# A three-layer feature-interaction tower on one core: the row sums of layer 2 taken from VectorE and made by ScalarE's accumulator, 16 columns at a time

## Chip, cores and metric

The kernel runs on one core of one Trainium2 chip. The metric is the device time of one execution in microseconds (us), median of the runs shown. All data are 32-bit floats.

## The reference, cut to what matters

For 1024 samples, 32 embeddings of 16 numbers are gathered from 32 tables (`e`, 1024 x 32 x 16). Three layers follow, each made of products of `e` with the layer before, contracted with a weight tensor. Each layer gives one sum over the 16 numbers (`d`) of its relu to a small MLP.

```python
    x0 = embeddings; xk = x0; outs = []
    for W in (W0, W1, W2):
        xk = jax.nn.relu(jnp.einsum('bmd,bhd,mhk->bkd', x0, xk, W))   # k = 64 maps
        outs.append(jnp.sum(xk, axis=2))
    z = jnp.concatenate(outs, axis=1)                 # 1024 x 192
    h = jnp.concatenate([z, dense_ctx], axis=1)       # 1024 x 208
    h = jnp.maximum(h @ W_top1 + b_top1, 0.0)         # 512
    h = jnp.maximum(h @ W_top2 + b_top2, 0.0)         # 256
    y = h @ W_top3
```

Layer 2 is the last of the three: its relu is not used again, only its sums are.

## The kernel before

The columns are the 1024 x 16 pairs (sample, number), worked in 16 steps of 1024 columns (64 samples). Half a step is 512 columns (32 samples, HALF_B), the width of one PSUM bank.

**Gather and spread.** GpSimd (POOL) gathers the embeddings of step s+2 during step s (`gather`, L247). SyncE (SP) stores them to HBM as rows (`store_rows`, L187), waits for the store, and then loads, on one queue, `x0g` of that step (L197) and 16 tiles `x0bc` of 128 x 1024 (L214, two tiles a semaphore). They go round in 24 slots.

**A layer.** For each of 16 tiles an elementwise product with the layer before is made, by VectorE for two tiles at once (L286, 128 x 2048) or, for the last 3 tiles of layers 1 and 2, by POOL (L260). TensorE contracts the products into one PSUM bank of 128 x 512 (`y_ps`, L413: the upper and lower 64 rows are the two halves of the step). Two such banks alternate. Layer 0 has only 4 tiles, and the squares made by ScalarE (L360). VectorE's products go through a ring of four (`prod`); the wait for a free place is `products_used`.

**After a layer** (`finish` on ScalarE, ACT): for layers 0 and 1, four copies of the relu to PSUM for VectorE (L370), the relu of the whole bank into SBUF (L374, 128 x 512), and four copies to SBUF for POOL (L379). For layer 2 only L374 runs. VectorE then makes the sums: `sums(s, l)`, one reduction of 128 x 512 to 128 x 32 (L314).

**Order written out by hand.** On VectorE, in step s: layer 1 of s; layer 0 of s+1; sums of layer 0 of s; sums of layer 2 of s-1; layer 2 of s; sums of layer 1 of s. On TensorE: layer 1 of s, layer 0 of s+1, layer 2 of s. On ScalarE: `place_x0g(s+1)` (L355, which waits for the load of x0g, and for which VectorE's layer 0 waits), `square(s+1)` (L360), `finish(s,1)`, `finish(s+1,0)`, `finish(s,2)`. On POOL, in step s: 3 tiles of layer 1 and 3 of layer 2, with 16 gathers between them. In the last two steps POOL takes 5 and 4 tiles.

**End.** `mlp_input(c)` on VectorE copies the sums of 8 steps into place with six copies (L326). The MLP jobs run on TensorE (L466, L467, L473) and ScalarE (L388 to L392) in the order of `MLP`: jobs (1,0,j) before layer 2 of the last step, and after it (2,0,0), (2,0,1), (1,1,0) to (1,1,3), and the rest. The jobs (1,1,j) wait for `mlp_input(1)`. On ScalarE all jobs after the first four stand behind `finish(LAST, 2)`.

Of the kernel before, what the change touches and what calls it, by code (L numbers as in the profile page):

```python
# [8 lines left out]
ACT = mybir.ActivationFunctionType  # L9
# [5 lines left out]
DIM = 16  # L15
# [12 lines left out]
HALF_B = STEP_B // 2  # L28
# [27 lines left out]
def groups_of(s, l):  # L56
    tiles = list(range(TILES - POOL_COUNT[s][l - 1])) if l else list(range(LOW))
    return [tiles[i:i + GROUP] for i in range(0, len(tiles), GROUP)]
# [7 lines left out]
def before(x):  # L66

    return sum(len(groups_of(*y)) for y in STAGES[:NUMBER[x]])


def after(x):
    return before(x) + len(groups_of(*x))
# [15 lines left out]
LAST = STEPS - 1  # L88


def slot(s, j):
    return (TILES * s + j) % SLOTS


def cin_tower_kernel(nc, table, ids, id_offset, dense_t, w0_a, w0_b, w0_sq, w1, w2,
                     wt1_a, wt1_b, bt1, wt2, bt2, wt3, x0_rows, out):
    with ExitStack() as ctx:
        def sb(name, shape, dt=F32):
            return ctx.enter_context(nc.sbuf_tensor(name, shape, dt))
# [4 lines left out]
        def sem(name):  # L104
            return ctx.enter_context(nc.semaphore(name))
# [16 lines left out]
        relu = sb("relu", [P, 3, HALF])  # L122
        z = sb("z", [P, 3, STEPS * HALF_B])
# [45 lines left out]
        relu_done = [sem(f"relu{l}_done") for l in range(3)]  # L169
# [6 lines left out]
        def y_bank(x):  # L176
            return y_ps[NUMBER[x] % 2]
# [100 lines left out]
        @block.vector  # L278
        def _(dve):
            def product(n, count, tiles, x, h=None):  # L280

                if n >= RING and h != 1:
                    dve.wait_ge(products_used, n - RING + 1)
                cols = slice(0, PAIR) if h is None else slice(HALF * h, HALF * (h + 1))
                right = x[:].rearrange("p h c -> p (h c)")[:, cols]
                made = dve.tensor_tensor(prod[:, n % RING, 0:count, cols], tiles[:, :, cols],  # L286
                                         right.unsqueeze(1).to_broadcast([P, count, right.shape[1]]), ALU.mult)
                if h != 0:
                    made.then_inc(products, 1)

            def layer0(s):
                dve.wait_ge(x0g_placed, s + 1)
                for g, group in enumerate(groups_of(s, 0)):
                    dve.wait_ge(bc_in[g], 32 * (s + 1))
                    at = slot(s, group[0])
                    product(before((s, 0)) + g, GROUP, x0bc[:, at:at + GROUP, :], x0g_ps)

            def layer(s, l, x):
                for g, group in enumerate(groups_of(s, l)):
                    if l == 1:  # L300
                        dve.wait_ge(bc_in[g], 32 * (s + 1))
                    n, at, count = before((s, l)) + g, slot(s, group[0]), len(group)
                    tiles = x0bc[:, at:at + count, :]
                    if g == 0:

                        for h in range(2):
                            dve.wait_ge(spread_done[l - 1], 4 * s + 2 * h + 2)
                            product(n, count, tiles, x, h)
                    else:
                        product(n, count, tiles, x)  # L310

            def sums(s, l):
                dve.wait_ge(relu_done[l], s + 1)
                dve.tensor_reduce(z[:, l, s * HALF_B:(s + 1) * HALF_B],  # L314
                                  relu[:, l, :].rearrange("p (b d) -> p b d", d=DIM), AX_X,
                                  ALU.add).then_inc(summed[l], 1)

            def mlp_input(c):
                steps = STEPS // 2
                for l in range(3):  # L320
                    dve.wait_ge(summed[l], steps * (c + 1))
                for l, dst in enumerate((zt_a[0:MAPS, :], zt_a[MAPS:P, :], zt_b[0:MAPS, :])):
                    dst = dst[:, HALF * c:HALF * (c + 1)].rearrange("p (s h b) -> p s h b", h=2, b=HALF_B)
                    for h in range(2):
                        src = z[MAPS * h:MAPS * (h + 1), l, steps * HALF_B * c:steps * HALF_B * (c + 1)]
                        dve.tensor_copy(dst[:, :, h, :],  # L326
                                        src.rearrange("p (s b) -> p s b", b=HALF_B)).then_inc(zt_ready, 1)

            dve.wait_ge(weights_in, 16 * 5)
            dve.tensor_tensor(w0s_sb[:], w0a_in, w0b_in, ALU.add).then_inc(w0_ready, 1)  # L330

            dve.tensor_scalar(wsq_sb[:], wsq_in, 1.0 / QUART, None, ALU.mult).then_inc(w0_ready, 1)

            layer0(0)
            for s in range(STEPS):
                layer(s, 1, x1_ps)
                if s < LAST:
                    layer0(s + 1)
                sums(s, 0)
                if s > 0:  # L340
                    sums(s - 1, 2)
                if s == LAST:
                    mlp_input(0)
                layer(s, 2, x2_ps)
                sums(s, 1)
            sums(LAST, 2)
            mlp_input(1)

        @block.scalar
        def _(act):  # L350
            def place_x0g(s):
                act.wait_ge(x0g_in, 16 * (s + 1))
                if s > 0:
                    act.wait_ge(products, after((s - 1, 0)))
                act.activation(x0g_ps[:].rearrange("p h c -> p (h c)"), x0g[:], ACT.Copy).then_inc(x0g_placed, 1)  # L355

            def square(s):
                if s > 0:
                    act.wait_ge(squares_used, s)
                act.activation(squares[:], x0g[:], ACT.Square).then_inc(squared, 1)  # L360

            def finish(s, l, x=None, x_sb=None):

                ps = y_bank((s, l))

                act.wait_ge(products_used, after((s, l)))
                if x is not None:
                    for h in range(2):
                        for copy in range(2):
                            act.activation(x[MAPS * copy:MAPS * (copy + 1), h, :], ps[MAPS * h:MAPS * (h + 1), :],  # L370
                                           ACT.Relu).then_inc(spread_done[l], 1)
                if s > 0:
                    act.wait_ge(summed[l], s)
                act.activation(relu[:, l, :], ps[:], ACT.Relu).then_inc(relu_done[l], 1)  # L374
                if x is not None:
                    act.wait_ge(relu_done[l], s + 1)
                    for h in range(2):
                        for copy in range(2):
                            act.activation(x_sb[MAPS * copy:MAPS * (copy + 1), HALF * h:HALF * (h + 1)],  # L379
                                           relu[MAPS * h:MAPS * (h + 1), l, :], ACT.Copy).then_inc(copied[l], 1)  # L380

            def mlp(jobs):
                for n in jobs:
                    layer, c, j = MLP[n]
                    act.wait_ge(mlp_mm, n + 1)
                    ps = mlp_ps[n % MLP_BANKS]
                    if layer == 1:
                        act.activation(h1[:, j, :], ps, ACT.Relu, bias=bt1_sb[:, j:j + 1]).then_inc(mlp_act, 1)  # L388
                    elif layer == 2:
                        act.activation(h2[:, j, :], ps, ACT.Relu, bias=bt2_sb[:, j:j + 1]).then_inc(mlp_act, 1)  # L390
                    else:
                        act.activation(y_sb[:, HALF * c:HALF * (c + 1)], ps[0:1, :], ACT.Copy).then_inc(mlp_act, 1)  # L392

            place_x0g(0)
            square(0)
            finish(0, 0, x1_ps, x1_sb)
            for s in range(STEPS):
                if s < LAST:
                    place_x0g(s + 1)
                    square(s + 1)  # L400
                finish(s, 1, x2_ps, x2_sb)
                if s < LAST:
                    finish(s + 1, 0, x1_ps, x1_sb)
                else:
                    mlp(range(MLP_EARLY))
                finish(s, 2)
            mlp(range(MLP_EARLY, len(MLP)))

        @block.tensor
        def _(pe):  # L410
# [6 lines left out]
            def wait_bank(x):  # L417

                n = NUMBER[x]
                if n >= 2:  # L420
                    s, l = STAGES[n - 2]
                    pe.wait_ge(relu_done[l], s + 1)

            def layer0(s):
                wait_bank((s, 0))
# [107 lines left out]
```

## Time and profile before

| | us |
|---|---|
| median of 3 runs | 644.31 (643.63 to 645.4) |
| the profiled execution | 642.9 |
| its span, first to last instruction | 641.1 |
| VectorE busy in it | 558.1 |
| TensorE busy in it | 559.1 |
| GpSimd busy in it | 488.4 |
| ScalarE busy in it | 224.6 |

The span lies inside the profiled execution's own time; 1.8 us lie around it. The median is 1.4 us above that execution. Shares of busy time are means over a filling part at the start (the first gathers), a repeating middle of about 35 us a step, and the MLP at the end, so the middle and the end have to be read apart.

### The profile page before, as it was taken

Reading aid. Unit: us, or ns where it says so; the run is one execution under the profiler, and the core shown is the slowest. Engines: PE = TensorE matmul, PEld = TensorE weight load, DVE = VectorE, ACT = ScalarE, POOL = GpSimd, SP = SyncE. Lnnn points to the kernel's source line nnn. Section 1 sums busy time; section 2 is a strip of 40 time slices with the busy share of each in tenths; the row PEclk is TensorE's granted clock in tenths of the full one; section 3 lists DMA queues with packets and bytes.
Section 4 is the critical chain, followed back from the end, with each engine's and each line's share of the span. In section 5 each row is a group of like instructions: output and inputs, shape, how many; then the busy total and the mean of one; then the engine's idle time right before and its main releaser. Section 6 shows DMA issues by size and latency. Waiting matters only on the chain.

```text
span 641.1 us, 6648 instructions
## 1 busy us (share of the span) xinstructions
PE 559.1 (87%) x2440; PEld 179.6 (28%) x2440; DVE 558.1 (87%) x346; ACT 224.6 (35%) x351; POOL 488.4 (76%) x364
## 2 busy tenths in 40 slices
PE   0047998999999998999999899999899999989998
PEld 0012232332323232323232232222232233323342
DVE  0047998999999999999999999999999999898810
ACT  0032607053341616160524425161606143340422
POOL 6756798879888888978788888888797979675500
PEclk9998999999999999999999999999999999999999
DMA  3298857677876758676778778675767687772000
GB/s 104 45 384 299 305 189 291 242 297 266 305 271 246 272 206 297 235 288 222 294 267 298 267 260 288 225 280 214 294 232 282 253 300 265 295 268 72 1 0 0
DMA packets 52835, 150.94 MB, mean 235 GB/s; under 512 B 9697, under 2 KB 17377, under 8 KB 52802
## 3 DMA queue, kind: packets, MB, share of 16 engines
q1 hardware_dynamic: 44610, 148.40, 62.8%
q0 software_dynamic: 8192, 2.11, 2.5%
q8 instruction: 19, 0.31, 0.2%
q14 instruction: 14, 0.11, 0.0%
HBM read 147.33 MB, written 3.15 MB: 235 GB/s over the span
## 4 chain that ended last, share of the span: by engine, by line
DVE 47%; DMA 16%; PE 15%; issue 13%; POOL 7%; SPq 2%; ACT 0%; DVEq 0%; POOLq 0%
DVE prod L286 43%; DMA x0bc<-x_rows 12%; PE y_ps L413 10%; POOL emb L247 6%; DVE z L314 4%; PE x0g_ps L473 2%; DMA x_rows<-emb 2%; DMA emb<-table,row_sb 2%; SPq L214 1%; PE x_ps L473 1%; POOL pool_prod L260 1%; PE x0g_ps L466 1%; PE x0g_ps L467 1%; PE x_ps L467 1%; PE x_ps L466 1%
## 5 line engine op out<-in xcount | busy, mean ns | idle before, releaser
L286 DVE TENSOR_TENSOR prod<-x0bc,x_ps 128x2048 f32<-128x2048 f32 (+1 forms) x252 | 456.2, 1879 | 8.6 <-ACT x_ps L370 7.2
L413 PE MATMUL y_ps<-prod,w_sb 128*64 128x512 f32 x1640 | 383.2, 597 | 36.6 <-DVE prod L286 36.6
L247 POOL DMA_INDIRECT emb<-table,row_sb x256 | 245.0, 957 | 65.4 <-issue 63.4
L260 POOL TENSOR_TENSOR pool_prod<-x0bc,x_sb 128x1024 f32<-128x1024 f32 x102 | 242.3, 2381 | 50.4 <-ACT x_sb L379 39.3
L413 PEld LDWEIGHTS y_ps<-prod,w_sb 128*64 128x64 f32 x1640 | 115.2, 137 | 287.3 <-issue 225.4
L413 PE MATMUL y_ps<-pool_prod,w_sb 128*64 128x512 f32 x408 | 105.1, 595 | 5.1 <-POOL pool_prod L260 5.1
L370 ACT ACTIVATE x_ps<-y_ps 64x512 f32<-64x512 f32 x128 | 73.0, 570 | 87.8 <-PE y_ps L413 85.2
L286 DVE TENSOR_TENSOR prod<-x0bc,x0g_ps 128x2048 f32<-128x2048 f32 x32 | 72.3, 2281 | 34.6 <-DMA x0bc<-x_rows 31.0
L379 ACT ACTIVATE x_sb<-relu 64x512 f32<-64x512 f32 x128 | 80.4, 628 | 3.4
L374 ACT ACTIVATE relu<-y_ps 128x512 f32<-128x512 f32 x48 | 28.7, 597 | 147.1 <-PE y_ps L413 146.3
L355 ACT ACTIVATE x0g_ps<-x0g 128x1024 f32<-128x1024 f32 x16 | 16.4, 1028 | 156.9 <-DMA x0g<-x_rows 156.9
L413 PE MATMUL y_ps<-prod,w0s_sb 128*64 128x512 f32 x256 | 60.3, 611 | 1.5 <-DVE prod L286 1.4
L413 PE MATMUL y_ps<-squares,wsq_sb 128*64 128x512 f32 x64 | 17.4, 623 | 35.6 <-ACT squares L360 35.6
L413 PEld LDWEIGHTS y_ps<-pool_prod,w_sb 128*64 128x64 f32 x408 | 29.0, 137 | 64.9 <-issue 51.7
L314 DVE TENSOR_REDUCE z<-relu 128x32 f32<-128x512 f32 x48 | 31.2, 675 | 6.4 <-ACT relu L374 6.4
L413 PEld LDWEIGHTS y_ps<-prod,w0s_sb 128*64 128x64 f32 x256 | 18.3, 140 | 41.7 <-issue 29.7
L413 PEld LDWEIGHTS y_ps<-squares,wsq_sb 128*64 128x64 f32 x64 | 4.6, 141 | 44.2 <-issue 44.2
L360 ACT ACTIVATE squares<-x0g 128x1024 f32<-128x1024 f32 x16 | 16.7, 1041 | 0.0
L473 PE MATMUL x0g_ps<-x0bc 128*128 128x512 f32 x24 | 10.7, 596 | 0.0
L330 DVE TENSOR_TENSOR w0s_sb<-pool_prod 128x256 f32<-128x256 f32 x1 | 0.4, 425 | 8.5 <-DMA w_sb<-w 8.5
L473 PEld LDWEIGHTS x0g_ps<-x0bc 128*128 128x128 f32 x24 | 4.5, 190 | 6.1 <-issue 6.1
L390 ACT ACTIVATE x0bc<-x0g_ps,bt_sb 128x512 f32<-128x512 f32 x3 | 2.1, 688 | 8.5 <-PE x0g_ps L473 8.5
(27 smaller groups left out, 45.4 us busy)
## 6 DMA issues: line engine op xcount, KB each, us to landing
x0bc<-x_rows SPq DMA_DIRECT2D x256, 512.0 KB, 6.6
x0g<-x_rows SPq DMA_DIRECT2D x16, 512.0 KB, 4.7
emb<-table,row_sb POOLq DMA_INDIRECT x256, 5.0
x_rows<-emb SPq DMA_DIRECT2D x16, 128.0 KB, 2.1
w_sb<-w SPq DMA_DIRECT2D x2, 512.0 KB, 4.5
x_rows<-emb SPq DMA_DIRECT2D x16, 64.0 KB, 2.0
x0bc<-wt SPq DMA_DIRECT2D x1, 512.0 KB, 5.3
x0bc<-wt_a SPq DMA_DIRECT2D x1, 256.0 KB, 4.0
```

The costliest lines, as they stand in the source:

```text
L247: pool.indirect_dma_start(emb[:, turn, DIM * n:DIM * (n + 1)], None, table, bass.IndirectOffsetOnAxis(row_sb[:, at:at + 1], 0)).then_inc(g ...
L260: pool.tensor_tensor(pool_prod[:, n % POOL_RING, :], x0bc[:, slot(s, j), :], x[:], ALU.mult).then_inc(pool_products, 1)
L286: made = dve.tensor_tensor(prod[:, n % RING, 0:count, cols], tiles[:, :, cols], right.unsqueeze(1).to_broadcast([P, count, right.shape[1]] ...
L314: dve.tensor_reduce(z[:, l, s * HALF_B:(s + 1) * HALF_B], relu[:, l, :].rearrange("p (b d) -> p b d", d=DIM), AX_X, ALU.add).then_inc(summ ...
L355: act.activation(x0g_ps[:].rearrange("p h c -> p (h c)"), x0g[:], ACT.Copy).then_inc(x0g_placed, 1)
L360: act.activation(squares[:], x0g[:], ACT.Square).then_inc(squared, 1)
L370: act.activation(x[MAPS * copy:MAPS * (copy + 1), h, :], ps[MAPS * h:MAPS * (h + 1), :], ACT.Relu).then_inc(spread_done[l], 1)
L374: act.activation(relu[:, l, :], ps[:], ACT.Relu).then_inc(relu_done[l], 1)
L379: act.activation(x_sb[MAPS * copy:MAPS * (copy + 1), HALF * h:HALF * (h + 1)], relu[MAPS * h:MAPS * (h + 1), l, :], ACT.Copy).then_inc(cop ...
L413: made = pe.matmul(ps[MAPS * h:MAPS * (h + 1), :], w, moving[:, HALF * h:HALF * (h + 1)], start=first, stop=final)
L466: pe.matmul(ps, wt1a_sb[:, out_f], zt_a[:, b], start=True, stop=False)
L473: made = pe.matmul(ps[0:rows, :], w[:, k, :], x[:, k, :], start=k == 0, stop=k == ks - 1)
```

## The change

VectorE's 16 reductions of layer 2 are taken out. ScalarE no longer makes one relu of 128 x 512 for layer 2; it makes 32 relus of 128 x 16, each of one sample's 16 columns, and each also writes the sum of its columns to one column of `z` (`accum_out`). The waits that counted one relu a step count 32 for layer 2, and the wait of layer 2's relu for VectorE's last sum falls away.

```diff
             def mlp_input(c):
                 steps = STEPS // 2
-                for l in range(3):
+                for l in range(2):
                     dve.wait_ge(summed[l], steps * (c + 1))
+                dve.wait_ge(relu_done[2], HALF_B * steps * (c + 1))
...
                 sums(s, 0)
-                if s > 0:
-                    sums(s - 1, 2)
                 if s == LAST:
                     mlp_input(0)
                 layer(s, 2, x2_ps)
                 sums(s, 1)
-            sums(LAST, 2)
             mlp_input(1)
...
+                if l == 2:
+
+                    for b in range(HALF_B):
+                        act.activation(relu[:, l, DIM * b:DIM * (b + 1)], ps[:, DIM * b:DIM * (b + 1)], ACT.Relu,
+                                       accum_out=z[:, l, s * HALF_B + b:s * HALF_B + b + 1]).then_inc(relu_done[l], 1)
+                    return
                 if s > 0:
                     act.wait_ge(summed[l], s)
                 act.activation(relu[:, l, :], ps[:], ACT.Relu).then_inc(relu_done[l], 1)
...
-                    pe.wait_ge(relu_done[l], s + 1)
+                    pe.wait_ge(relu_done[l], (HALF_B if l == 2 else 1) * (s + 1))
```

## Rows read from the trace of the kernel before

**Rows 1.** The page: span, and busy time of each engine.

```profile
span 641.1 us, 6648 instructions
PE 559.1 (87%) x2440; PEld 179.6 (28%) x2440; DVE 558.1 (87%) x346; ACT 224.6 (35%) x351; POOL 488.4 (76%) x364
```

**Rows 2.** Timeline of VectorE, one middle step (start, length in us, engine, line).

```profile
314.64 1.27 DVE L314 TENSOR_REDUCE z<-relu 128x32 f32<-128x512 f32 x2
315.83 14.46 DVE L286 TENSOR_TENSOR prod<-x0bc,x_ps 128x1024 f32<-128x1024 f32 x8
...
330.80 14.46 DVE L286 TENSOR_TENSOR prod<-x0bc,x_ps 128x1024 f32<-128x1024 f32 x8
345.33 4.68 DVE L286 TENSOR_TENSOR prod<-x0bc,x0g_ps 128x2048 f32<-128x2048 f32 x2
```

**Rows 3.** Timeline of ScalarE, the same step; in brackets the idle time before.

```profile
312.74 2.35 ACT L370 ACTIVATE x_ps<-y_ps 64x512 f32<-64x512 f32 x4 [4.34 <-PE y_ps L413]
...
332.70 0.60 ACT L374 ACTIVATE relu<-y_ps 128x512 f32<-128x512 f32 x1 [8.76 <-PE y_ps L413]
341.40 1.03 ACT L355 ACTIVATE x0g_ps<-x0g 128x1024 f32<-128x1024 f32 x1 [8.10 <-DMA x0g<-x_rows]
```

**Rows 4.** ScalarE's instructions grouped: busy us, mean ns of one, idle before.

```profile
L379 ACT ACTIVATE x_sb<-relu 64x512 f32<-64x512 f32 x128 | 80.4, 628 | 3.4
...
L374 ACT ACTIVATE relu<-y_ps 128x512 f32<-128x512 f32 x48 | 28.7, 597 | 147.1 <-PE y_ps L413 146.3
L360 ACT ACTIVATE squares<-x0g 128x1024 f32<-128x1024 f32 x16 | 16.7, 1041 | 0.0
```

**Rows 5.** SyncE's queue: the loads of x0bc that follow a store.

```profile
337.25 5.18 SPq L214 DMA_DIRECT2D x0bc<-x_rows  x6
```

**Rows 6.** Chain that ended last, around 345 us: a load.

```profile
339.19 8.50 DMA x0bc<-x_rows
```

**Rows 7.** Line L214, third and fourth load: first of the twelve steps.

```profile
L214 SPq DMA_DIRECT2D x0bc<-x_rows x2: 588/726/863, 128.3 to 128.9; - x2
...
DMA to landing us min/median/max: 7.2/7.7/8.2
```

**Rows 8.** The same, last of the twelve steps.

```profile
L214 SPq DMA_DIRECT2D x0bc<-x_rows x2: 602/656/709, 513.9 to 514.6; - x2
...
DMA to landing us min/median/max: 6.6/7.0/7.3
```

**Rows 9.** Timeline of GpSimd: its first tile of layer 2.

```profile
318.41 2.37 POOL L260 TENSOR_TENSOR pool_prod<-x0bc,x_sb 128x1024 f32<-128x1024 f32 x1 [1.26 <-ACT x_sb L379]
```

**Rows 10.** Timeline of TensorE: the start of layer 2.

```profile
318.31 1.94 PE L413 MATMUL y_ps<-prod,w_sb 128*64 128x512 f32 x8 [1.33 <-DVE prod L286]
```

**Rows 11.** Timeline of VectorE: last two steps.

```profile
555.75 2.29 DVE L286 TENSOR_TENSOR prod<-x0bc,x0g_ps 128x2048 f32<-128x2048 f32 x1 [2.35 <-issue]
...
593.55 13.40 DVE L286 TENSOR_TENSOR prod<-x0bc,x_ps 128x1024 f32<-128x1024 f32 x7 [2.83 <-ACT x_ps L370]
```

**Rows 12.** Timeline of the end: ScalarE.

```profile
613.32 0.60 ACT L374 ACTIVATE relu<-y_ps 128x512 f32<-128x512 f32 x1 [12.91 <-PE y_ps L413]
```

**Rows 13.** Timeline of the end: VectorE.

```profile
613.95 0.69 DVE L314 TENSOR_REDUCE z<-relu 128x32 f32<-128x512 f32 x1 [6.40 <-ACT relu L374]
614.77 1.88 DVE L326 COPY x0bc<-z 64x256 f32<-64x256 f32 x6
```

**Rows 14.** Timeline of the end: TensorE.

```profile
613.20 7.13 PE L473 MATMUL x0g_ps<-x0bc 128*128 128x512 f32 x16
620.17 1.02 PE L466 MATMUL x_ps<-x0bc 128*128 128x512 f32 x2
```

**Rows 15.** TensorE early in the kernel, after an idle stretch.

```profile
55.67 1.50 PE L413 MATMUL y_ps<-pool_prod,w_sb 128*64 128x512 f32 x4 [3.66 <-POOL pool_prod L260]
56.94 3.22 PE L413 MATMUL y_ps<-prod,w_sb 128*64 128x512 f32 x8
```

**Rows 16.** Busy time and TensorE's granted clock (PEclk, after POOL) in two stretches there.

```profile
57.00:58.00 1.00, 1.00 (x6) 0.39 (x4) 1.00 (x1) 0.00 (x0) 1.00 (x1) 0.50 0.81 49
...
60.00:61.00 1.00, 1.00 (x8) 0.42 (x6) 0.72 (x1) 0.12 (x1) 0.98 (x2) 1.00 0.99 352
```

## The prediction

> **What bounds the kernel now.** I read the page first: VectorE and TensorE are both busy 87% of the 641.1 us span, ScalarE 35% [rows 1]. Two engines look equal there, so the next view is the timeline of one middle step on VectorE. It shows products, sums and products again with no gap: from 315.83 the layer-2 products last to 330.29, the layer-1 products run 330.80 to 345.26, layer 0 starts at 345.33 [rows 2]. TensorE in the same step idles 1.33 us before layer 2, waiting for VectorE's product [rows 10]. So VectorE sets the pace in the middle, and the work that the change removes stands in its queue. ScalarE idles 8.10 us between the relu of layer 2 and the placing of x0g, for which it waits on a load [rows 3].
>
> VectorE is not alone, though. The chain that ended last runs at 345 us through a load of x0bc of 8.50 us, issued at 339.19 and landed at 347.69 [rows 6], 0.2 us after VectorE could have used it: the second of its two layer-0 products would have started at 345.33 + 2.20 = 347.53 (two of them take 4.68 us instead of the usual 4.47 [rows 2]). The loads of a step start only when POOL's gathers are stored [rows 5], and POOL starts that series when ScalarE hands it x_sb [rows 9]. So a second loop, POOL, store, load, runs just beside VectorE.
>
> At the end, TensorE runs MLP jobs from 613.20 to 620.17 while ScalarE and VectorE finish layer 2 by 616.65 [rows 12 to 14]: 3.52 us of cover.
>
> **Removed from VectorE, middle.** Two sums in a row take 1.27 us, and products start 1.19 us after the first of them; a lone one takes 0.69 and would give 0.60 [rows 2, 13]. So one removed sum brings the layer-2 products 0.59, say 0.6 us, forward. Fifteen sums go before the last step's end. Which of them lie on the path?
> - The one of step 15 (before the products of 593.55) does not: VectorE idles 2.83 us there for x_ps [rows 11]. Gain 0.
> - The one of step 13 does not: the layer 0 after it already idles 2.35 us before 555.75 [rows 11], called issue, but the second load of that step lands just then. It is late by the second loop, whose start lies before the removed sum. Gain 0.
> - The one of step 14 does: TensorE is next, and it waits for VectorE at that place as in [rows 10]. 0.6.
> - Twelve are left, steps 1 to 12: 12 x 0.6 = 7.2 us at best.
>
> **What the second loop takes back.** x_sb, with which POOL's series starts, comes from layer 1, whose products precede the removed sum. So POOL, stores and loads are not 0.6 us earlier when VectorE is, and the margin of the fourth load before the second layer-0 product shrinks by 0.6 in each step. In the first of the twelve steps it lands at 128.9 + 8.2 = 137.1 [rows 7] with the product at 137.6, a margin of 0.5; in the last at 514.6 + 7.3 = 521.9 [rows 8] with the product at 522.8, 0.9. The twelve, worked out the same way: 0.5, 0.5, 0.8, -0.1, 0.7, 0.7, -0.2, 0.3, 0.3, -0.3, 0.7, 0.9. Where the margin is under 0.6 only the margin is gained: 0.5 + 0.5 + 0.6 + 0 + 0.6 + 0.6 + 0 + 0.3 + 0.3 + 0 + 0.6 + 0.6 = 4.6. A stall in one step leaves the next margin larger by its length, since x_sb precedes the stall; followed through the twelve, this gives back up to 0.7 (5.3). I take 5.0, with step 14 **5.6 us gained**. Ends: 7.8 if the loads come earlier too, 3 if they jitter more. POOL keeps up: of its 1.26 us of idle [rows 9] 0.6 goes.
>
> **Added on ScalarE: what one small relu costs.** No row shows a 16-column activation or one with its sum written out. From 512 to 1024 columns an SBUF activation goes from 628 to 1041 ns, 0.81 ns a column [rows 4]; the PSUM relu of 512 takes 597 ns [rows 4], so 16 columns take 597 - 496 x 0.81 = 195 ns. Four copies take 2.35 us [rows 3], some 20 ns apart beyond their length. A small relu alone: at least 0.2 us. The written-out sum is a single column that can only go out when the 16 are through. Nothing excludes that it hides in the gap (0), and as a second instruction it can hardly cost more than a small activation of its own (0.2). So one costs 0.2 to 0.41 us, and 32 cost 6.6 to 13.1. Between them I take half an instruction, 0.3 us, **9.6 us for 32**: one column is less than a full small activation, but a write that follows another has never been free in these rows.
>
> The row shows that 512 columns cost 597 ns, of which 180 or so are fixed [rows 4]; cut in 32 the fixed part is paid 32 times. The Trainium skill says the same against this change (Advanced Engine Details and Errata, The Read-Write Bubble): large tiles of 512 or 1024 elements, because latency shows between instructions. On the size it differs: by ScalarE: Activation LUTs (What ACT_TABLE_LOAD costs) 16 columns take 186 + 13 = 199 ns with immediate operands, and consecutive activations overlap by 93, which would make it an estimate of 106 ns each and 3.4 us for 32. The rows above show no overlap, only gaps.
>
> **Beside what it lies in the middle.** From 332.70 ScalarE is idle, but for the 0.6 us relu, until 341.40 [rows 3]: 8.7 us. 9.6 puts the placing of x0g at 342.4 instead, its end (1.03 later) at 343.4. VectorE needs it at 345.33 [rows 2]. So up to 345.3 - 1.1 - 332.7 = 11.5 us (0.36 each) cost nothing; queued behind it are the placing, the square and finish(s,1), whose PSUM bank is full only about 15 us after the relu (4.34 us of idle before 312.74 [rows 3]). TensorE's own wait for the bank of layer 2 comes later than the square, so it is behind the same work. Cost 0.
>
> **Added at the end.** After 613.32 stand 32 relus instead of 0.60 us of relu and 0.69 of sum [rows 12, 13]. Then the six copies, 1.88 us and 0.1 of waiting: the sums are in place at 613.3 + 9.6 + 2.0 = 624.9. The jobs (1,1,j) started at 620.17 [rows 14]. The cover of 3.52 us is used up, **4.7 us lost**. In general 32p - 4.9, with p the cost of one.
>
> TensorE idles these 4.7 us. Early in the kernel it idled 3.66 us [rows 15] and then ran at a granted clock of 0.50 (1.2 GHz), with 1.00 (2.4 GHz) again by 60 us [rows 16]; 8 matmuls took 3.22 us where they take 1.94 [rows 10, 15], and four 1.50 where they take 1.03: 1.8 us in all. The end is a chain through TensorE, so I add **1.8 us lost**. (The Trainium skill, TensorE: Matmul & The Clock Gate, states that idleness halves the array's clock until work has gone on for a time; the trace agrees with its 0.50.)
>
> **The sum.** -5.6 + 4.7 + 1.8 = +0.9 us. The profiled execution took 642.9, so 643.8; the median shown is 1.4 above it, so 644.3 + 0.9 = **645.2 us**. That is within 0.3% (1.9 us), about what a measurement of this kernel can tell from no change.
>
> **Rivals.**
> - *ScalarE becomes the bound (slower).* If one costs over 0.36 us, the placing of x0g is late in every step and layer 0 with it. At 0.37 (11.8 us) it is 0.3 to 0.4 late each step, the gain falls from 5.6 to about 2.5, the end costs 6.9 + 1.8: +6, 650.5. At 0.41 it is 1.6 us late, net of the removed sum 1.0 in each of twelve steps, and 10.1 at the end: +22, 666. For it: two dependent writes an activation. Against: it needs more than three quarters of a full instruction for the sum.
> - *The small ones are cheap (faster).* At 0.2 us, 6.6 for 32, the end costs 1.7, the idle stretch is too short to resemble [rows 15], and the gain of 5.6 stands: -3.9, 640.4. The overlap that the skill states is this rival's rule taken further; at that price the end would lie wholly in cover and the time would be 638.7.
> - *The gain does not come.* If the loads' loop takes back nearly all (gain 1.0), the end's 6.5 stands: +5.5, 649.8. For it: three of twelve margins are below zero already. Against: five are 0.7 or more.
> - That the sums stay on VectorE is excluded by the diff.
>
> **From these to the numbers.** The forecast 0.45 (one costs 0.25 to 0.36; 643 to 647), ScalarE bound 0.22, cheap 0.2, no gain 0.13. The range reaches from the cheap case, 640.4, to past the milder bound case, 651. Faster: the cheap case and a little of the forecast's edge, less its weak part, 0.2. Slower: bound, no gain, and little else, 0.36. Same 0.44.
>
> **What the changed kernel's profile would show.** On ScalarE, 512 activations of 128x16, and perhaps as many rows for the sums: the stretch from the first to the last of a step should be 9.6 us. VectorE should have 32 reductions, steps of about 34.5 us instead of 34.94, and more idle time on x0bc loads (about 2.5 us more). TensorE should idle 4 to 5 us before the first matmul of (1,1,0), with the clock at 0.5 behind it. The placing of x0g should follow the last small relu without a gap. Wrong would be: a stretch of under 8 or over 11.5 us; idle time on VectorE before layer 0 that ends with the placing; a clock that stays at 1.00 at the end (1.8 us less).

## The result, and the profile after

The changed kernel takes 638.83 us (median of 4 runs, 638.44 to 639.81) against 644.86 of the kernel before, run beside it: ratio 0.991, 95% interval 0.989 to 0.993, 4 to 7 us faster. Its profiled execution took 638.9, with a span of 637.1, against 642.9 and 641.1: 4.0 us less in this pair. I had forecast 645.2 and no measurable change; the time lies below the whole range.

The page first: its span, and busy time by engine.

```profile
span 637.1 us, 7625 instructions
...
PE 563.1 (88%) x2440; PEld 178.9 (28%) x2440; DVE 548.7 (86%) x330; ACT 302.5 (47%) x1359; POOL 488.3 (77%) x364
```

VectorE has 16 instructions and 9.4 us less than in [rows 1]. ScalarE has 1008 more: 496 relus, and 512 of a kind that was not there. Its groups (busy us, mean ns of one, idle before):

```profile
L373 ACT ACTIVATION_READ_ACCUMULATOR relu<-y_ps 128x1 f32 x512 | 84.7, 315 | 0.2
L373 ACT ACTIVATE relu<-y_ps 128x16 f32<-128x16 f32 x512 | 84.5, 287 | 144.3 <-PE y_ps L417 144.3
```

So the sum is a second instruction. The means of 287 and 315 ns mislead. The timeline of ScalarE shows it (start, length):

```profile
296.60 0.17 ACT L373 ACTIVATE relu<-y_ps 128x16 f32<-128x16 f32 x1
296.66 0.19 ACT L373 ACTIVATION_READ_ACCUMULATOR relu<-y_ps 128x1 f32 x1
296.75 0.17 ACT L373 ACTIVATE relu<-y_ps 128x16 f32<-128x16 f32 x1
...
301.28 0.41 ACT L373 ACTIVATE relu<-y_ps 128x16 f32<-128x16 f32 x1
301.34 0.44 ACT L373 ACTIVATION_READ_ACCUMULATOR relu<-y_ps 128x1 f32 x1
305.38 1.03 ACT L353 ACTIVATE x0g_ps<-x0g 128x1024 f32<-128x1024 f32 x1 [3.61 <-DMA x0g<-x_rows]
```

Each row starts before the one ahead of it has ended, and the rows grow longer, from 0.17 to 0.44 us, while the distance from one relu to the next stays 0.155. What counts is the distance of the starts: 0.06 to the read, 0.09 to 0.10 to the next relu. For the step that answers to [rows 3], line L373 between 325 and 340 us:

```profile
L373 ACT ACTIVATE relu<-y_ps x32: 165/284/413, 331.8 to 336.8; 128x16 f32<-128x16 f32 x32
L373 ACT ACTIVATION_READ_ACCUMULATOR relu<-y_ps x32: 192/311/441, 332.0 to 336.9; 128x1 f32 x32
```

From 331.8 to 336.9 + 0.44, the end of the last row, are 5.5 us for all 32, not 9.6. The placing of x0g still waits for its load, 2.89 us after them, in place of 8.10:

```profile
340.18 1.03 ACT L353 ACTIVATE x0g_ps<-x0g 128x1024 f32<-128x1024 f32 x1 [2.89 <-DMA x0g<-x_rows]
```

VectorE, two products of layer 0 and what follows (answers to [rows 2]):

```profile
308.52 2.28 DVE L286 TENSOR_TENSOR prod<-x0bc,x0g_ps 128x2048 f32<-128x2048 f32 x1
312.13 2.29 DVE L286 TENSOR_TENSOR prod<-x0bc,x0g_ps 128x2048 f32<-128x2048 f32 x1 [1.32 <-DMA x0bc<-x_rows]
314.33 0.68 DVE L314 TENSOR_REDUCE z<-relu 128x32 f32<-128x512 f32 x1
314.93 14.46 DVE L286 TENSOR_TENSOR prod<-x0bc,x_ps 128x1024 f32<-128x1024 f32 x8
```

One sum now, and products 0.60 us after it; but 1.32 us of idle before the second product, which waits for a load. VectorE's waits between 100 and 540 us (total, times, longest), first of the kernel before:

```profile
DVE prod L286 <- DMA x0bc<-x_rows: 1.0, 2, 0.8
DVE prod L286 <- issue: 0.9, 1, 0.9
```

and of the changed kernel:

```profile
DVE prod L286 <- DMA x0bc<-x_rows: 5.5, 7, 1.9
DVE prod L286 <- issue: 1.0, 2, 0.7
```

A wait called issue stands before the same products, with no releaser named; I count it with the loads, as in the prediction. So 6.5 us of idle in place of 1.9 in this pair, 4.6 us more. Single executions differ in this, though. In the same stretch the trace of a kernel with all sums on VectorE and small relus added has 4.2 us, and three further traces with layer 2's sums gone from VectorE have 5.3, 4.9 and 4.5 us (all from the experiments below; traces of the first job, disturbed as told there, are left out). Two executions with the sums on VectorE have 3.1 us in the mean, four without them 5.3: 2.2 us more.

The end, TensorE first (answers to [rows 14]), then VectorE (to [rows 13]):

```profile
608.46 7.13 PE L477 MATMUL x0g_ps<-x0bc 128*128 128x512 f32 x16
616.10 1.10 PE L470 MATMUL x_ps<-x0bc 128*128 128x512 f32 x2 [0.51 <-DVE x0bc L327]
```

```profile
614.07 1.88 DVE L327 COPY x0bc<-z 64x256 f32<-64x256 f32 x6 [11.27 <-ACT relu L373]
```

TensorE enters the MLP's last part 4.74 us earlier than before (608.46 against 613.20), and waits 0.51 us in it, not 4.7. Of the 4.74, 0.74 was there before any sum was removed: the products of step 0's layer 2 start at 68.38 us, in the kernel before at 69.12. Over the traces of this study that start lies anywhere from 67.8 to 71.7 us. Its granted clock there (the figure 1.00 behind the busy times):

```profile
616.00:620.00 4.00, 3.90 (x9) 1.81 (x10) 0.00 (x0) 1.19 (x3) 0.00 (x0) 1.00 0.00 0
```

### The profile page after: what moved, and what is told of

The parts are those of the page before. It is cut to its first block, busy times and chain, and to the rows that moved or that the text cites. A ratio compares the mean times of both kernels' runs of the same rounds, so it can differ in the third digit from the quotient of the medians.

```text
span 637.1 us, 7625 instructions
## 1 busy us (share of the span) xinstructions
PE 563.1 (88%) x2440; PEld 178.9 (28%) x2440; DVE 548.7 (86%) x330; ACT 302.5 (47%) x1359; POOL 488.3 (77%) x364
## 4 chain that ended last, share of the span: by engine, by line
DVE 36%; PE 24%; DMA 19%; issue 10%; POOL 8%; SPq 2%; ACT 1%; DVEq 0%; POOLq 0%
DVE prod L286 34%; PE y_ps L417 20%; DMA x0bc<-x_rows 15%; POOL emb L247 6%; DVE z L314 2%; DMA emb<-table,row_sb 2%; DMA x_rows<-emb 2%; POOL pool_prod L260 1%; SPq L214 1%; PE x_ps L477 1%; ACT relu L373 1%; PE x0g_ps L477 1%; PE x_ps L470 1%; PE x0g_ps L470 1%; PE x0g_ps L471 1%
## 5 line engine op out<-in xcount | busy, mean ns | idle before, releaser
L260 POOL TENSOR_TENSOR pool_prod<-x0bc,x_sb 128x1024 f32<-128x1024 f32 x102 | 242.3, 2382 | 45.7 <-ACT x_sb L383 36.3
L373 ACT ACTIVATE relu<-y_ps 128x16 f32<-128x16 f32 x512 | 84.5, 287 | 144.3 <-PE y_ps L417 144.3
L373 ACT ACTIVATION_READ_ACCUMULATOR relu<-y_ps 128x1 f32 x512 | 84.7, 315 | 0.2
L417 PE MATMUL y_ps<-prod,w0s_sb 128*64 128x512 f32 x256 | 61.6, 617 | 5.4 <-DVE prod L286 5.4
L314 DVE TENSOR_REDUCE z<-relu 128x32 f32<-128x512 f32 x32 | 21.6, 676 | 0.0
L378 ACT ACTIVATE relu<-y_ps 128x512 f32<-128x512 f32 x32 | 19.1, 597 | 0.8
L327 DVE COPY x0bc<-z 64x256 f32<-64x256 f32 x12 | 3.4, 286 | 11.6 <-ACT relu L373 11.3
L477 PE MATMUL x0g_ps<-x0bc 128*128 128x512 f32 x24 | 10.7, 597 | 0.0
```

Source lines behind the costliest of these rows:

```text
L260: pool.tensor_tensor(pool_prod[:, n % POOL_RING, :], x0bc[:, slot(s, j), :], x[:], ALU.mult).then_inc(pool_products, 1)
L314: dve.tensor_reduce(z[:, l, s * HALF_B:(s + 1) * HALF_B], relu[:, l, :].rearrange("p (b d) -> p b d", d=DIM), AX_X, ALU.add).then_inc(summ ...
L373: act.activation(relu[:, l, DIM * b:DIM * (b + 1)], ps[:, DIM * b:DIM * (b + 1)], ACT.Relu, accum_out=z[:, l, s * HALF_B + b:s * HALF_B + ...
L417: made = pe.matmul(ps[MAPS * h:MAPS * (h + 1), :], w, moving[:, HALF * h:HALF * (h + 1)], start=first, stop=final)
L477: made = pe.matmul(ps[0:rows, :], w[:, k, :], x[:, k, :], start=k == 0, stop=k == ks - 1)
```

## Experiments

Ratios are to the kernel before, run on the same chip in the same job, with their 95% intervals. The changed kernel's is 0.991. The edits are to the changed kernel unless another is named.

### The addition and the removal, each alone

**Nobody sums layer 2.** ScalarE makes one relu of 128x512 as before, the MLP reads layer 1's sums twice.

```diff
-                    for b in range(HALF_B):
-                        act.activation(relu[:, l, DIM * b:DIM * (b + 1)], ..., accum_out=z[...])
+                    act.activation(relu[:, l, :], ps[:], ACT.Relu).then_inc(relu_done[l], 1)
...
-                        src = z[MAPS * h:MAPS * (h + 1), l, ...]
+                        src = z[MAPS * h:MAPS * (h + 1), min(l, 1), ...]
```

> Leaves work out: nobody sums layer 2; ScalarE makes one relu of 128x512, and the MLP gets layer 1's sums in place of layer 2's. It is the removal from VectorE without the addition to ScalarE. Theory A (the small relus are covered by ScalarE's idle time in the middle and cost only what sticks out of TensorE's MLP jobs at the end, 0.5 us): within 1.5 us of the changed kernel, 637 to 639 us, middle steps alike, with VectorE idle 4 to 7 us on loads of x0bc between 100 and 540 us. Rival B (the small relus cost something in the middle too, for example by the later placing of x0g): 3 us or more faster than the changed kernel.

0.991 (0.988 to 0.995), in a job where the kernel before itself took 646.6. Repeated in another job:

> The kernel in which nobody sums layer 2 (the MLP gets layer 1's sums in its place), once more. Theory A: 0 to 1.5 us less than the changed kernel, 637 to 639 us. Rival B: 635 us or less; then the small relus cost 3 us or more in the changed kernel.

637.05 us, 0.990 (0.987 to 0.993). Both ratios are the changed kernel's. So the 512 small relus with their sums cost nothing that can be told from none.

**The small relus added, VectorE's sums kept** (edit to the kernel before):

```diff
+                if l == 2:
+                    for b in range(HALF_B):
+                        act.activation(relu[:, l, DIM * b:DIM * (b + 1)], ps[:, DIM * b:DIM * (b + 1)], ACT.Relu,
+                                       accum_out=z_acc[:, b:b + 1]).then_inc(relu_done[l], 1)
+                    return
```

> The kernel before, with layer 2's relu made as 32 relus of 16 columns whose sums are written out into a tile that nobody reads; VectorE still makes the sums. It is the addition to ScalarE without the removal from VectorE. Theory A (5.0 us, covered in the middle; at the end 613.2 + 5.1 + 0.8 + 1.9 = 621.0 against 620.2): +0.5 to +1.5 us, not to be told from the kernel before. Rival B (the small relus slow something else in the middle): +3 us or more.

1.000 (0.999 to 1.002). At the end of its profile TensorE waits, as expected:

```profile
625.45 1.10 PE L472 MATMUL x_ps<-x0bc 128*128 128x512 f32 x2 [1.23 <-DVE x0bc L327]
```

So the gain is the removal's.

**Small relus without a sum written out** (the kernel before with `accum_out` left away in the edit above):

> The kernel before with layer 2's relu cut into 32 relus of 16 columns without an accumulator; VectorE still makes the sums. It shows the price of a small relu alone. Theory A (a relu and the writing out of its sum take 0.156 us from one to the next, of which 0.09 is the relu): 32 take about 3 us; the middle does not change; the end has 613.3 + 3.0 + 0.8 + 1.9 = 619 against 620.2, still covered; time as before, within 1 us. Rival B (consecutive activations overlap only when an accumulator write stands between them; alone each takes the 0.195 us of my prediction): 32 take 6.2 us, and the end is 2 us later, +2 us.

1.001 (0.998 to 1.003). Line L376 in one step:

```profile
L376 ACT ACTIVATE relu<-y_ps x32: 178/372/578, 338.5 to 340.5; 128x16 f32<-128x16 f32 x32
```

31 distances in 2.0 us (2.0 to 2.1 in the steps at 89, 125, 161 and 197 us too): one relu each 0.065 us, less than the 0.09 that theory A gave it and a third of the 0.195 of my prediction. The last row ends at 341.1, 2.6 us after the first start. The Trainium skill (ScalarE: Activation LUTs, What ACT_TABLE_LOAD costs) has back-to-back activations overlap, an estimate of 106 ns for 16 columns: right in direction, and the measured 65 ns decides. The gap between instructions that the Trainium skill holds against small tiles (Advanced Engine Details and Errata, The Read-Write Bubble) does not show in these rows, which overlap. Large tiles are cheaper all the same: the 32 take 2.6 us, one relu of 512 columns 0.60 [rows 4].

### The end

```diff
-                if l == 2:
+                if l == 2 and s < LAST:
...
+            dve.wait_ge(relu_done[2], HALF_B * LAST + 1)
+            dve.tensor_reduce(z[:, 2, LAST * HALF_B:], relu[:, 2, :].rearrange("p (b d) -> p b d", d=DIM), AX_X,
+                              ALU.add).then_inc(summed[2], 1)
             mlp_input(1)
```

> The changed kernel, with step 15's layer 2 done the old way: one relu of 128x512, then VectorE's reduction. Theory A (32 relus at the end cost only what exceeds TensorE's cover, 0.5 us): TensorE goes into the jobs (1,1,j) without a wait, the profile's stretch from the last matmul of layer 2 to the end is 0.4 to 0.6 us shorter; the time is 0 to 1 us less, not to be told from the changed kernel. Rival B (the 5 us of relus count in full at the end): 4 us less.

637.85 us, 0.990 (0.987 to 0.994), not to be told from the changed kernel. In the profile TensorE no longer waits:

```profile
608.72 7.13 PE L483 MATMUL x0g_ps<-x0bc 128*128 128x512 f32 x16
615.69 1.02 PE L476 MATMUL x_ps<-x0bc 128*128 128x512 f32 x2
```

From 608.72 to the end of the span, 636.6, are 27.9 us, as before the change (613.20 to 641.1), against 28.6 in the changed kernel (608.46 to 637.1). The end costs 0.7 us, not 6.5. The timed runs cannot show so little, but the traces agree: from the start of VectorE's last products of layer 2 to the end are 47.5 to 47.6 us in the kernel before, here and where nobody sums, and 48.3 in the changed kernel and its copy with one increment a step (below).

### How much ScalarE could take

My cover of 11.5 us a step in the middle was not tested by 5 us of work. So the relus were made again into tiles that nobody reads, in steps 0 to 14 (`range(2)` in the tripled kernel):

```diff
+                    if s < LAST:
+                        for r in range(1):
+                            for b in range(HALF_B):
+                                act.activation(relu_more[:, r, DIM * b:DIM * (b + 1)], ps[:, DIM * b:DIM * (b + 1)],
+                                               ACT.Relu, accum_out=z_more[:, r, b:b + 1]).then_inc(relu_done[l], 1)
```

**Doubled:**

> The changed kernel with layer 2's 32 relus and sums made twice in steps 0 to 14 (the second time into tiles that nobody reads), once in step 15. Theory A (cover of 11.5 us in the middle): 64 take 10.0 us, the placing of x0g comes 1 to 2 us later than in the changed kernel and still before VectorE needs it; time unchanged within 1.5 us. Rival B (the cover is the 8.1 us until x0g lands, and what exceeds it shows): 1 to 1.5 us a step, +15 to +20 us.

1.007 (1.003 to 1.012), 10 us above what the changed kernel's ratio would give, and neither theory's number.

**Tripled:**

> The same three times, 96 relus and sums, 15.0 us. Theory A: 3.5 us over the cover of 11.5 in each of some 14 steps, less the idle time on loads that it swallows (5 us): VectorE waits before layer 0 for the placing of x0g, +40 to +49 us, 680 to 688. Rival B (cover 8.1): 7 us a step, +95. Rival C (other work moves into the gap, so less shows): under +30.

787.3 us, 1.217: no theory's number either. ScalarE's timeline there shows pauses among the relus:

```profile
285.17 0.19 ACT L380 ACTIVATION_READ_ACCUMULATOR relu_more<-y_ps 128x1 f32 x1
285.74 0.18 ACT L380 ACTIVATE relu_more<-y_ps 128x16 f32<-128x16 f32 x1 [0.37 <-issue]
286.44 0.20 ACT L380 ACTIVATION_READ_ACCUMULATOR relu_more<-y_ps 128x1 f32 x1 [0.52 <-issue]
```

Rows that had followed at 0.155 us a pair now came at about 0.7. I took the semaphore increments, one a relu, for the cause, and left one a step, behind the loop:

```diff
-                    ... accum_out=...).then_inc(relu_done[l], 1)
+                    made = act.activation(..., accum_out=...)
+                    made.then_inc(relu_done[l], 1)
```

> The kernel with layer 2's relus and sums made three times in steps 0 to 14, but with one semaphore increment a step, at the last relu, in place of 96. In the run with 96 increments ScalarE went from 0.156 us a pair to 0.7 us a pair after some 70 pairs, and the time was 787 us. Theory A (the increments' way is what backs up): all 96 pairs go at 0.156, 15.0 us, and the time is the 680 to 688 us expected for the cover of 11.5 us. Rival B (the supply of instructions to ScalarE is what runs dry, or the writes of one column): the pauses stay, 780 us or more.

> The same two times, one increment a step. Theory A: 10.0 us, inside the cover of 11.5 us: the time of the changed kernel, 637 to 641 us, and no late copies to PSUM for layer 2. Rival B: as the doubled kernel with all increments, 650 us or more.

Tripled 699.3 us, 1.083 (1.082 to 1.085); doubled 638.6, 0.991 (0.989 to 0.994). That looked like proof, but the two pairs had run in different jobs. The same kernels with all increments, repeated:

> The kernel that makes layer 2's relus and sums three times in steps 0 to 14, each with its own semaphore increment, once more in another job. Theory A (96 increments in a row back up whatever the chip): 780 us or more again, with ScalarE's pauses of 0.35 to 1.2 us. Rival B (that job's chip was the cause): about 699 us, as with one increment a step.

> The kernel that makes them three times, a third time. Theory A: 697 to 701 us; the 787 us was of that one job. Rival B: about 787 us again; then the kernel has two ways to run.

> The kernel that makes layer 2's relus and sums twice in steps 0 to 14, each with its own increment, once more. Theory A (the first job's chip delayed it; the cover is 11.5 us): 637 to 641 us, as with one increment a step. Rival B (the increments delay it): 648 us or more again.

698.8 (1.085, 1.083 to 1.088) and 699.6 (1.086, 1.082 to 1.090) tripled; 637.6 (0.991, 0.988 to 0.994) doubled. So the increments alone were not the cause, and my theory fell; a kernel with one increment was not run in the first job. The pauses belonged to that job, in which the kernel before was slower too (646.6 against 643.6 to 644.9 in the others). Nor was it a matter of small relus alone. In the four traces of that job ScalarE's first copies to PSUM, before any small relu, start at 48.9 to 49.9 us, in all others at 43.7 to 45.7. The record gives chip 1 for this job and for that of the 699.3 us. What delayed ScalarE there stays open; of that job only the two ratios near 1 that were repeated or that agree with others are used here, and the 65 ns a relu.

**One increment a step in the changed kernel itself:**

> The changed kernel with one semaphore increment a step for layer 2's relus in place of 32. Theory A (32 never back up): the changed kernel's time, within 1 us, 0.155 us a pair. Rival B (they cost something already): 2 us or more faster.

638.8, 0.992 (0.990 to 0.995): no effect.

With the disturbance gone, the cover is seen. The tripled kernel with one increment, line L378, and VectorE before layer 0:

```profile
L378 ACT ACTIVATE relu_more<-y_ps x64: 435/616/617, 328.0 to 338.3; 128x16 f32<-128x16 f32 x64
L378 ACT ACTIVATION_READ_ACCUMULATOR relu_more<-y_ps x64: 463/642/645, 328.1 to 338.4; 128x1 f32 x64
L378 ACT ACTIVATE relu<-y_ps x32: 167/290/426, 322.8 to 327.9; 128x16 f32<-128x16 f32 x32
```

```profile
340.10 4.49 DVE L288 TENSOR_TENSOR prod<-x0bc,x0g_ps 128x2048 f32<-128x2048 f32 x2 [4.70 <-ACT x0g_ps L355]
```

From 322.8 to 338.4 + 0.64 are 16.2 us, and 16.2 - 11.5 = 4.7: the idle time of VectorE, which ends with the placing of x0g (4.7 to 5.0 in the middle steps). The doubled relus, 10.7 us in the trace with one increment (329.4 to 340.1), fit and cost nothing. The 699 us is more than the 680 to 688 expected because 96 relus take 16.2, not 15.0 us.

### Where the rest of the gain went

**One gather moved ahead of POOL's tiles of layer 2**, in the changed kernel and in the one before:

```diff
-GATHERS_AFTER = {1: [1, 1, 8], 2: [1, 1, 4]}
+GATHERS_AFTER = {1: [1, 1, 9], 2: [1, 1, 3]}
```

> The changed kernel with one gather moved ahead of POOL's tiles of layer 2 in each step (9 and 3 in place of 8 and 4), so that the store and the loads of a step start up to 1.25 us earlier. Theory A (what was not gained in the middle, 2 to 5 us, was taken back by the loop of gathers, stores and loads): VectorE's idle time on x0bc loads between 100 and 540 us falls from 6.5 us to under 2; 3 to 4.5 us faster than the changed kernel. Rival B (POOL itself has only 0.65 us of idle left, so the gather moved ahead delays its tiles and x_sb's use by 0.6, and TensorE waits for POOL's products): under 1.5 us faster or slower, with new waits of TensorE on POOL. Rival C (the loads are late by transfer speed, not by their start): no change of that idle time.

634.8 us, 0.985 (0.983 to 0.988), 4 us under the changed kernel's 638.8. VectorE's waits between 100 and 540 us:

```profile
DVE prod L286 <- DMA x0bc<-x_rows: 2.5, 2, 1.9
DVE prod L286 <- issue: 0.3, 1, 0.3
```

2.8 us in place of 6.5, and less than in any of the four traces named above (4.5 to 6.5): in the changed kernel VectorE does wait for the loop of gathers, store and loads. (I had expected under 2.)

> The same move of one gather in the kernel before. Theory A: there VectorE idles only 1.9 us on loads between 100 and 540 us, so 1 to 2 us at most are gained, which the measurement can't tell from none. Rival B: the same gain as in the changed kernel, 3 us or more; then the second loop bounded the kernel before as well.

641.8, 0.996 (0.994 to 0.998), 2.4 us less: between the two theories. Its profile has 3.3 us of such idle in that stretch, not less than before, so where its gain sits is not shown. And since the same move gives 2.4 us here and 4 us there, with intervals wider than the difference, the times do not show how much of the 4 us the removed sums had lost to the loop.

**Layer 0's sums by ScalarE too**, behind the copies to POOL:

```diff
-                sums(s, 0)
...
+                if l == 0:
+                    for b in range(HALF_B):
+                        act.activation(relu_out[:, DIM * b:DIM * (b + 1)], relu[:, 0, DIM * b:DIM * (b + 1)], ACT.Relu,
+                                       accum_out=z[:, 0, s * HALF_B + b:s * HALF_B + b + 1]).then_inc(summed[0], 1)
```

> The changed kernel, with layer 0's sums made by ScalarE too: 32 relus of 16 columns of the relu in SBUF, behind the copies to POOL, with their sums written out; 0.6 us less for VectorE in each step. Theory A (ScalarE has 9.5 us idle there and 5 are used; but what VectorE gains after layer 0 is taken back by the loads, as in the changed kernel, where margins are used up): 0 to 3 us faster, with VectorE's idle time on loads up from 6.5 to 11 us or more between 100 and 540 us. Rival B (each removed sum counts in full): 9 us faster.

635.3, 0.986 (0.983 to 0.988), 3.5 us less, where 9 us of sums were removed. VectorE's idle on loads rises to 10.5 us (expected were 11 or more):

```profile
DVE prod L287 <- issue: 6.1, 8, 1.6
DVE prod L287 <- DMA x0bc<-x_rows: 4.4, 9, 1.3
```

**Both:**

> The changed kernel with both further edits: layer 0's sums by ScalarE and one gather moved ahead of POOL's tiles of layer 2. Theory A (each of the two alone gave 3.5 to 4 us; together VectorE's shorter step meets loads that start earlier): faster than either, 629 to 632 us. Rival B (POOL, with 33.7 us of work a step, becomes the bound): 633 us or more, with POOL idle under 0.3 us a step.

626.8, 0.972 (0.971 to 0.974): 12 us under the changed kernel, more than 4 + 3.5 and better than the 629 to 632 expected. I read it so: with layer 0's sums gone too, VectorE runs into the loads (10.5 us of idle), and the gather moved ahead brings them earlier. The idle time on loads in that stretch is 4.3 us, and TensorE now waits for POOL:

```profile
PE y_ps L421 <- POOL pool_prod L261: 7.1, 12, 0.7
PE y_ps L421 <- DVE prod L287: 6.4, 30, 0.6
```

**All that paid, with the old end and one increment a step:**

> Everything that paid in one kernel: layers 2 and 0 summed by ScalarE with one increment a step, one gather moved ahead of POOL's tiles of layer 2, and the last step's layer 2 the old way. Theory A: as with layer 0 and the gather alone (626.8 us), and 0.5 us less at the end: 625 to 627 us. Rival B (increments of two layers a step already backed up there): under 624 us.

626.4 us, 0.973 (0.971 to 0.975): as the one above; the best two of the study, not to be told apart.

## Why the prediction was wrong

**The step that failed** is "Added on ScalarE: what one small relu costs". It took 0.3 us, from a range of 0.2 to 0.41; measured are 0.155. Even the lower bound was too high, since it said that a small relu alone takes at least 0.2 us. That came from the length of a row, 195 ns, and from four long copies that lie end to end; I called the fixed part, some 180 ns, paid 32 times. The runs show that a small relu's fixed part lies beside its neighbours: 65 ns from one to the next, and 90 more for the read of the sum. The rows of long activations could not show that, and the overlap that the Trainium skill states (ScalarE: Activation LUTs, What ACT_TABLE_LOAD costs) was put aside on their strength.

**What hung on it.** By the prediction's own formula the end costs 32p - 4.9: with p = 0.155 nothing (0.1), with what the last instructions take to finish about 0.5 us; measured 0.51 of waiting and 0.7 in the whole end. The 4.7 us were thus 4.0 too much, and the 1.8 us for the clock fell away with the idle stretch: TensorE waits 0.51 us and stays at 1.00. Both together are 5.8 us, most of the 6.4 between 645.2 and 638.8.

For the two profiled executions the account closes: forecast was 0.9 us more, measured 4.0 less, 4.9 apart. The end makes 5.8 of it and the earlier start 0.7 (luck, no part of the change); against them stands 1.6, since up to the end of layer 2 the removal gave 4.0 us (4.74 less 0.74), not 5.6. (A slip without effect: 332.70 + 9.6 is 342.3, not 342.4.)

**What held.**
- *One removed sum gives 0.6 us*: the products follow the lone sum by 0.60.
- *The second loop takes part of it back*: the direction was right, the size is not settled. I expected 2.2 us (7.2 less 5.0). The pair has 4.6 us of new idle time on loads, the mean of four traces against two 2.2. From step 0's layer-2 products to those of the last step the pair gains 4.0 us (524.4 to 520.4). The trace with all sums kept and small relus added has 527.1 there (the slowest of its ten executions), the three others without layer 2's sums 518.4 to 519.3. The forecast 5.6 lies inside this spread, and the timed runs, 4 to 7 us faster in all, allow it too.
- *Nothing in the middle up to 11.5 us of ScalarE*: 10.7 us cost nothing, 16.2 cost 4.7 a step.
- *POOL's idle falls by 0.6 us*: so it does in this step, where its first tile of layer 2 waits 0.65 us for x_sb in place of 1.26 [rows 9]. Over the 13 such waits between 100 and 540 us it is 14.2 us in place of 17.0, 0.2 a step; I take it that VectorE's waits for loads give POOL time back. The row of this step:

```profile
316.69 2.38 POOL L260 TENSOR_TENSOR pool_prod<-x0bc,x_sb 128x1024 f32<-128x1024 f32 x1 [0.65 <-ACT x_sb L383]
```

**The rivals.** It went the way of "the small ones are cheap", forecast at 0.2 with 640.4 for 0.2 us; at the measured price that rival's sum is -5.6 + 0.5 = -5.1, 639.2 with the median shown then. The 638.7 that the prediction gives at the price by that overlap, 106 ns, is nearer to the measured 638.83 than its reasons are: a relu with its sum takes 155 ns, the removal gave 4.0 us in the pair and not 5.6, and the kernel before ran at 644.86 beside it, not 644.31. "ScalarE becomes the bound" came true only in the tripled kernel. "The gain does not come" did not: the loads took part of it back, 2 to 5 us by the traces, and 4 to 7 us were left.

## What to carry to other kernels

The length of an instruction's row is not its price in a series: take the distance between starts, and if no row shows a series of that size, let the lower bound go under the length. A few microseconds of idle time read from one execution of each kernel can be chance: look at every trace of the same kind. An engine that idles 8 us a step can take reductions from the engine that sets the pace, at no cost until the idle time is used up; work out from the deadline of the next user how much that is. When the pace-setter gets faster, look for the loop that runs just beside it: here the gain of two small edits together was more than the sum of each.

## What I had not expected of the hardware

Small activations follow each other at 65 ns (128x16, PSUM to SBUF), and the read of the accumulator is an instruction of its own that adds 90 ns. And one kernel, the tripled one, took 787 us in one job and 699 in two others, with nothing changed; pauses of up to 1.2 us stood among ScalarE's small instructions there, 70.9 us in all. Why is open.
